# Attention row maxima: from columns into the query rows by DMA of 16-byte pieces, with query tiles of every fourth query

## What is computed

```
q = rope(x @ Wq + bq); k = rope(x @ Wk + bk); v = x @ Wv + bv      # 16 heads of 8 features
attn = softmax(q @ k.T / sqrt(8), axis=-1)                         # 1024 x 1024 per head and sequence
x = x + (attn @ v) @ Wo + bo
```

## Time and profile before

| | |
|---|---|
| median of 3 executions | 2727.1 us (2724.94 to 2729.11) |
| the profiled execution | 2726.42 us, span 2724.6 us |
| TensorE busy | 2199.8 us (81%), 17224 matmuls |
| VectorE busy | 2106.6 us (77%) |
| ScalarE busy | 1501.6 us (55%) |
| GpSimd busy | 473.7 us (17%) |
| granted clock, mean | 0.878 of 2.4 GHz |
| DMA of SP's queue | 55408 packets, 88.60 MB |

### The profile page before, as it was taken

One profiled execution on the slowest core, in us unless ns is written; L12 is line 12 of the kernel. 1 busy time (PEld: TensorE's weight loads), 2 busy tenths in 40 slices (PEclk: granted clock), 3 DMA queues, 4 the chain that ended last, 5 costly groups with the idle time before them and its releaser, 6 DMA issues. The chain is left out here.

```text
span 2724.6 us, 46987 instructions
## 1 busy us (share of the span) xinstructions
PE 2199.8 (81%) x17224; PEld 1193.6 (44%) x17224; DVE 2106.6 (77%) x4600; ACT 1501.6 (55%) x2898; POOL 473.7 (17%) x404
## 2 busy tenths in 40 slices
PE   6888963881479999999999669999999999449920
PEld 5667753770233333333333333333333333348920
DVE  6677667665569999999995668999999997375635
ACT  4433431240108888888888206888888888304510
POOL 2223310566420000000000120000000000006645
PEclk9889975895759999999999768999999999658965
DMA  4000000242330000000000330000000000202212
GB/s 178 0 0 0 0 17 22 64 91 68 111 129 26 14 26 14 26 23 17 26 2 2 108 129 14 26 14 25 26 14 26 14 14 2 94 14 62 69 49 55
DMA packets 64573, 109.69 MB, mean 40 GB/s; under 512 B 10352, under 2 KB 44272, under 8 KB 64112
## 3 DMA queue, kind: packets, MB, share of 16 engines
q1 hardware_dynamic: 55408, 88.60, 9.6%
q0 software_dynamic: 8960, 18.37, 3.1%
HBM read 64.46 MB, written 41.94 MB: 39 GB/s over the span
## 5 line engine op out<-in xcount | busy, mean ns | idle before, releaser
L1159 DVE TENSOR_REDUCE mh<-psum 128x1 f32<-128x512 f32 x2048 | 1253.9, 683 | 86.7 <-PE psum L1033 77.6
L1139 ACT ACTIVATE p<-psum 128x512 f32<-128x512 f32 x2048 | 1111.2, 596 | 204.1 <-PE psum L1067 166.7
L1033 PE MATMUL psum<-ks,qs 64*128 64x512 f32 x2048 | 766.6, 462 | 36.1 <-DMA ks<-qk_parts 35.4
L1067 PE MATMUL psum<-qs,ks 64*128 64x512 f32 x2048 | 749.3, 446 | 2.4 <-ACT p L1139 2.4
L1079 PE MATMUL psum<-p,v_ext 128*32 128x256 f32 x8192 | 655.7, 392 | 34.3 <-ACT p L1139 34.3
L1067 PEld LDWEIGHTS psum<-qs,ks 64*128 64x128 f32 x2048 | 303.7, 185 | 391.6 <-ACT p L1139 353.5
L1079 PEld LDWEIGHTS psum<-p,v_ext 128*32 128x32 f32 x8192 | 162.0, 108 | 412.4 <-issue 233.8
L1033 PEld LDWEIGHTS psum<-ks,qs 64*128 64x128 f32 x2048 | 312.3, 190 | 66.7 <-DMA ks<-qk_parts 35.8
L598 ACT ACTIVATE hid<-psum,stage 128x128 f32<-128x128 f32 x448 | 132.5, 367 | 180.7 <-PE psum L568 180.7
L542 POOL DMA_INDIRECT x_in<-n_rows,token_of x152 | 166.4, 1095 | 250.5 <-POOLq L78 183.4
L875 POOL TENSOR_TENSOR lo<-rot,hi 128x512 fp32r<-128x512 f32 x32 | 40.2, 1266 | 837.0 <-ACT hi L906 837.0
(11 more groups left out here) (190 smaller groups left out, 2154.5 us busy)
## 6 DMA issues: line engine op xcount, KB each, us to landing
qk_parts<-hi SPq DMA_DIRECT2D x32, 512.0 KB, 4.5
qs<-qk_parts SPq DMA_DIRECT2D x128, 100.0 KB
ks<-qk_parts SPq DMA_DIRECT2D x128, 100.0 KB
answers<-y_out SPq DMA_DIRECT2D x152, 64.0 KB, 1.6
qk_parts<-lo SPq DMA_DIRECT2D x16, 512.0 KB, 4.5
ew<-in_moe SPq DMA_DIRECT2D x1, 5136.0 KB, 18.3
ew<-in_moe SPq DMA_DIRECT2D x1, 4624.0 KB, 13.8
n_rows<-xn SPq DMA_DIRECT2D x8, 512.0 KB, 3.2
```

Of the source, the lines that this page charges most:

```text
L1033: pe.matmul(psum[:, bank, :], a["qs"][r, g % NKF, i * P:(i + 1) * P], a["ks"][r, g % NKF, j % KM, k * HALF:(k + 1) * HALF], start=True, st ...
L1067: pe.matmul(psum[:, S_BANK + n % NS, :], a["ks"][r, g % NKF, j % KM, i * P:(i + 1) * P], a["qs"][r, g % NKF, h * HALF:(h + 1) * HALF], sta ...
L1139: act.activation(a["p"][:, n % NP, :], psum[:, S_BANK + n % NS, :], ACT.Exp, scale=DH ** -0.5)\
L1159: dve.tensor_reduce(a["mh"][:, g % 2, c, k:k + 1], psum[:, bank, :], AX.X, ALU.max).then_inc(used, 1)
```

## The change

The turn of the maxima through TensorE and VectorE goes. A query tile is no longer 128 neighbouring queries but every fourth query of a half: tile i of half h is the queries 512h + i, 512h + i + 4, and so on. With that, the four columns of `mx` that one head has in a half hold, on partition p, the maxima of the four neighbouring queries 512h + 4p to 512h + 4p + 3. They are 16 bytes that stand together both in `mx` and in the row of `qs`, so four DMAs per half (one per head) move 128 such pieces each, from 128 partitions into one row. `mx` becomes float32r, SP waits for the merge, the score matmuls wait for four DMAs instead of one, and VectorE waits, ahead of each merge from the third group on, for the stores of the group two before, which has the same buffer. Scores, exponentials and products are as before.

```diff
     first = [("max", *divmod(u, UN), k) for u in range(LEAD) for k in range(2)]
-    first.insert(2 * UH + 4, ("turn_max", 0, 0, 0))
...
     for g in range(GROUPS):
-        for h in range(NH):
-            if g or h:
-                plan[STEPS * g + NT * h - 3].append(("turn_max", g, h, 0))
...
             def store_maxima(g, h):
-                sp.wait_ge(turned, NH * g + h + 1)
-                r = ROWS_QK - 1
-                sp.dma_start(a["qs"][r:P:GR, g % NKF, h * HALF:(h + 1) * HALF].bitcast(F32)
-                             .rearrange("r (i c) -> r i c", c=P), a["m_row"][:, h, :].bitcast(F32)).then_inc(row[h], 16)
+                sp.wait_ge(merged, NH * g + h + 1)
+                for j in range(GH):
+                    r, c = GR * j + ROWS_QK - 1, UH * h + TPH * j
+                    sp.dma_start(a["qs"][r:r + 1, g % NKF, h * HALF:(h + 1) * HALF].bitcast(F32)
+                                 .rearrange("r (p i) -> r p i", p=P),
+                                 a["mx"][:, g % 2, c:c + TPH].bitcast(F32)).then_inc(row[h], 16)
...
-                    pe.matmul(psum[:, bank, :], a["qs"][r, g % NKF, i * P:(i + 1) * P],
+                    pe.matmul(psum[:, bank, :], a["qs"][r, g % NKF, i // TPH * HALF + i % TPH:(i // TPH + 1) * HALF:TPH],
                               a["ks"][r, g % NKF, j % KM, k * HALF:(k + 1) * HALF], start=True, stop=True).then_inc(filled, 1)
-                elif kind == "turn_max":
-                    pe.wait_ge(merged, NH * g + u + 1)
-                    pe.transpose(psum[0:UH, bank, 0:P], a["mx"][:, g % 2, UH * u:UH * (u + 1)], t["ident"][:, :])\
-                        .then_inc(filled, 1)
...
-                    pe.wait_ge(row[h], 16 * (g + 1))
+                    pe.wait_ge(row[h], 16 * GH * (g + 1))
...
                         dve.wait_ge(used, n + 1 - sum(by_act[:n + 1]))
+                        if g >= 2:
+                            dve.wait_ge(row[h], 16 * GH * (g - 1))
                         dve.tensor_reduce(a["mx"][:, g % 2, UH * h:UH * (h + 1)], a["mh"][:, g % 2, UH * h:UH * (h + 1), :],
                                           AX.X, ALU.max).then_inc(merged, 1)
-                elif kind == "turn_max":
-                    if g:
-                        dve.wait_ge(row[u], 16 * g)
-                    dve.tensor_copy(a["m_row"][:, u, :], psum[0:UH, bank, 0:P]).then_inc(turned, 1)
-                    dve.wait_ge(turned, NH * g + u + 1)
-                    dve.sem_inc(used, 1)
...
-            a["mx"] = sb("mx", [P, 2, UN], where=both)
+            a["mx"] = sb("mx", [P, 2, UN], F32R, where=both)
-            a["m_row"] = sb("m_row", [UH, NH, P], F32R, where=both)
```

More of the change, by code:

```diff
@@ L966, in place @@
         return u // GH, units[u]
-    with stage(nc, "loaded0", "loaded1", "loaded2", "loaded3", "row0", "row1", "filled", "used", "turned",
+    with stage(nc, "loaded0", "loaded1", "loaded2", "loaded3", "row0", "row1", "filled", "used",
                "merged", "summed", "scored", "exped", "weighed", "out_copied", "recip", "o_copied") as \
-            (block, loaded0, loaded1, loaded2, loaded3, row0, row1, filled, used, turned,
+            (block, loaded0, loaded1, loaded2, loaded3, row0, row1, filled, used,
              merged, summed, scored, exped, weighed, out_copied, recip, o_copied):
```

## The result

The changed kernel takes **2833.5 us** (median of 4; 2832.5 to 2834.4) against 2727.2 for the kernel before on the same chip: ratio 1.039, 95% interval 1.0372 to 1.0408, 106.3 us more. The forecast was 2819 us with a range up to 2832: the direction and the main mechanism held, the size was missed by 14.5 us. The profiled execution has a span of 2830.7 us.

A forecast was written before the change was run, and what follows sets the result against it. TensorE was taken as the bound, VectorE close behind. Transposes -13.4, copies 0, DMAs 0 and strided weights +105.2 summed to +91.8 us on 2727.1, giving 2819 us, about 3.4% slower; range 2711 to 2832.

The forecast's parts named there:

- What bounds the kernel: Attention stages: TensorE first, busy 41.16 of 42.24 us per four-head group; VectorE 40.64, ScalarE 35.76.
- Part 1: 64 transposes leave TensorE: 13.0 us less in the loops, 0.4 ahead of them, together 13.4 us less.
- Part 2: 64 copies of 269 ns leave VectorE: worth nothing beyond the transposes' gain, as TensorE stays first.
- Part 3: Maxima sent by four DMAs of 16-byte pieces: about 8 us, inside 9.2 us of room, so zero cost.
- Rival D: Way of the maxima: 16-byte pieces land late, up to +1150 us, or +62 in a mild form; chance 0.03.
- Part 4: Maxima matmuls' weights, every fourth element: each load 0.106 us longer, 105 us more in all (77 by the smaller price).
- 976 x 0.106 = 103.5 us: Loops: each of 976 half-steps with maxima grows by the 0.106 us of its open strided load.
- rival B: Half-steps: the second, hidden strided load outlasts the first matmul and stalls too, 0.212 us per half-step, 2921 us; chance 0.04.
- Rival C: Half-steps: strided price partly hidden, 20 to 60 ns each, +6 to +45 us, 2733 to 2772; chance 0.09.
- The signs that the forecast named: Trace: maxima loads near 290 ns, half-step 1.33 to 1.34 us, second load 0.21 after first, group near 45 us.
- The further 1.7 us ahead of the loops: Between the warming matmuls: strided loads of 16 pairs add 1.7 us.
- Rival A: Weight port: strided columns read as fast as contiguous, only the transposes' gain counts, 2713.7 us; chance 0.36.

The follow-up runs named there:

- experiment 1: The changed kernel, but the maxima matmuls read 128 neighbouring queries (contiguous weights) again, 16-byte pieces kept: 2718.0 us, ratio 0.9971 to the kernel before.
- experiment 6: The changed kernel with only the first maxima matmul of each half-step reading every fourth query, the second contiguous: 2827.9 us, ratio 1.0376 to the kernel before.
- experiment 2: The kernel before, transposes and one DMA per half kept, with only the maxima matmuls reading every fourth query: 2840.4 us, ratio 1.0419.

## Why the prediction was right in kind and short in size

What bounds the kernel: right but for two half-steps of 32. TensorE set the pace before and after, and the 0.42 us of the turns came through in full. The loss came through in 30 of 32 half-steps of a group; in the other two TensorE waits for ScalarE, which hid it. ("Almost no idle time" ahead of the exponentials was too strong: the earlier trace rows has 204.1 us beside 1111.2 busy. The sum does not use it.)

Part 1, the transposes: right in the loops (0.42 us per group, 16 groups, 2 layers: 13.5 us), **wrong ahead of them**, where a term was left out. "The two turns before the loops stretch one period of the warming matmuls" took the turn for an insertion that leaves its neighbours alone. It set their parity. Instead of 0.4 us less, the stretch grew by 1.75 us per layer, 3.5 in all. The pair of periods in the earlier trace rows, 2.08 and 1.88, was read as one with and one without a turn; the period ahead of the turn, 799.80 to 802.10 in the same timeline, is 2.30 and would have shown it.

Part 2, the copies: right; VectorE had room.

Part 3, the DMAs: right, with room to spare (2.0 us to land where 3.4 had been taken from a larger transfer). Rival D falls: the 16-byte pieces stay in experiment 1, which is faster than before. The new wait of VectorE and the later loads of the queue appear in no list of waits of the changed kernel.

Part 4, the strided weights: the mechanism was right, and so was the load itself. The second load follows 0.21 us after the first, 0.104 more than before in the median of the half-steps; the forecast had 0.106. That it comes out as the 213 ns taken from VectorE's strided read was better than the evidence: the row is another engine's at another distance, and the prediction had 78 ns as its other price. That the row shows the stride's price at all needs one more row: line 463 also reads PSUM and line 465 does not. Line 1184 adds from PSUM and from contiguous SBUF in 692 ns, so the 1009 ns do not come from PSUM:

```profile
L1184 DVE TENSOR_TENSOR x_all<-psum,x_all 128x512 f32<-128x512 f32 x8 | 5.5, 692 | 4.3 <-PE psum L1055 4.3
```

**The step that failed is from the load to the half-step; the term was mis-sized.** "976 x 0.106 = 103.5 us" took the half-step to grow by what the load grows. It grows by 0.125 us, because the second maxima matmul starts 0.12 later (0.46 against 0.34) where its load starts 0.10 later, in experiment 6 too, where that second load is contiguous. What makes up this 0.02 us is open. It is paid in 30 of 32 half-steps: 976 x 30/32 x 0.125 = 114, for the 115.4 measured, or 0.118 per half-step on average, of which the open load has 0.113 and the hidden one, which "just fits beside the first matmul", 0.006. The forecast gave rival B only as a doubling; what happened is its mildest form. Rival C, a partly hidden price, holds in two half-steps of 32. The signs that the forecast named were off by the same step: a half-step of 1.36 us for 1.33 to 1.34, a group of 45.6 for 45.

The further 1.7 us ahead of the loops were close to nothing: there the granted clock is 0.50 (1.2 GHz), and the changed kernel's period of the warming matmuls is 2.32 us against 2.30, so that the stretch takes 37.1 us for 36.9. Of the changed kernel the stretch (us, busy PE, PEld, DVE, ACT, POOL, granted clock) and a period:

```profile
780.00:815.00 35.00, 34.65 (x62) 16.45 (x58) 28.44 (x48) 0.00 (x0) 0.00 (x0) 0.50 0.11 40
```

```profile
801.29 1.22 PE L1087 MATMUL psum<-y_t,att 128*128 128x256 f32 x2
...
803.61 1.22 PE L1087 MATMUL psum<-y_t,att 128*128 128x256 f32 x2
```

Together, against the forecast's +91.8: the loads +10 (115.4 for 105.2) and the parity +3.9 (+3.5 for -0.4) make +105.7; measured +106.3. That the two sides meet so closely is partly luck: experiment 1's 7.0 us of gain against 13.5 - 3.5 = 10 leaves 3 us unplaced, inside its interval (4.6 to 11.2). The profiled executions show one thing that varies by such amounts: TensorE's clock rises from 0.50 to its upper level only 6 to 9 us after the first score matmul, at another moment in each layer and execution. The text ahead of the prediction says of the warming matmuls that they keep the clock up; in no trace is it up while they run, and no run shows what they are worth.

The range missed by 1.5 us. Its upper end left 13 us above the 2819, and the mis-sized loads alone (+10, 2829 us) would have stayed inside; the lost gain ahead of the loops (+3.9) took it over the edge. Nothing made 1.66 ns per element, from another engine, an upper bound for what a half-step of TensorE pays.

Rival A, with over a third of the chance, fell by experiments 1 and 2: the change's gain without the stride is 7.0 us, and the stride alone costs 115.

## What to carry to other kernels

A weight tile read with a step cost here by the 16-byte lines that it opens: a step of two fp32 columns was nearly free (7 ns per half-step), steps of four and eight doubled the time from one load to the next (0.11 to 0.21 us). Where a load stood open on TensorE's path the half-step paid all of it and 0.02 us more; where it was hidden beside a matmul, or TensorE waited for another engine anyway, next to nothing. So count the open loads, and price them from the next matmul's start and not from the load alone. When pieces for a DMA are bought by such a step, take the smallest that the DMA's room allows: 8-byte pieces and twice the DMAs took back 108 of the 115 us that 16-byte pieces lost. And before an element is taken out of a hand-made order, look at what its place did to the neighbours: with alternating halves of the array, parity alone was worth 3 us per layer, close to half of the 13.4 us expected of the whole change in two layers.

## What the runs showed of the hardware that was not expected

Two engines read at the same price per line. VectorE's read of one element per line came at 1.66 ns, and TensorE's strided loads followed each other at 0.21 us for 128 columns, 1.66 ns per column (212 ns), though its contiguous loads (0.84 ns per column) are faster than VectorE's (1.05). That both meet the same limit is suggested by this and not shown.

At the lower clock the stride was nearly free: 0.02 us per period with two loads, against 0.118 per half-step at the higher. The strided load keeps its time: the second load follows 0.21 us after the first at either clock, while the contiguous one goes from 0.11 to 0.16 us at the lower. Of these 0.05 us the period shows only 0.02.

Two matmuls of 64 rows on one half of the array took a period 0.42 us longer, at the lower clock, than two on different halves (2.30 against 1.88).

DMAs of 128 pieces of 16 bytes, and of 8, both landed in 2.0 us (median; 1.9 to 3.7 for the former): halving the bytes from 2 KB to 1 KB per DMA did not matter.
